# A message-passing network on one core: one of four one-hot comparisons of a unit is made by GpSimd instead of VectorE

## The reference, cut to what matters

```python
def gcn_conv(x, edge_index, W, b):
    xw = x @ W.T
    deg = jax.ops.segment_sum(jnp.ones_like(dst, dtype=x.dtype), dst, num_segments=n)
    dinv = jnp.where(deg > 0, jax.lax.rsqrt(deg), 0.0)
    norm = dinv[src] * dinv[dst]
    msg = xw[src] * norm[:, None]
    out = jax.ops.segment_sum(msg, dst, num_segments=n)
    return out + b
```

## Time and profile before

| | |
|---|---|
| median of three runs | 5927.08 us |
| the profiled execution | 5925.47 us, span 5923.7 us |
| the stage `build_counts_and_sum` | from 138.2 to 771.7 us, 633.5 us |
| VectorE, TensorE, ScalarE, GpSimd busy over the whole span | 55%, 55%, 41%, 39% |
| granted clock of TensorE over the span | 0.749 of full speed |

### The profile page before, as it was taken

The page is one execution under the profiler, slowest core; times in us unless marked ns, Lnnn a source line. Parts: engine busy times, 40 slices in busy tenths (PEclk is TensorE's granted clock), DMA queues, the critical chain, the costliest instruction groups (busy, mean ns, idle before and its releaser), DMA issues. The chain is left out here.

```text
span 5923.7 us, 64720 instructions
## 1 busy us (share of the span) xinstructions
PE 3257.2 (55%) x16208; PEld 1977.8 (33%) x16208; DVE 3247.8 (55%) x10115; ACT 2411.6 (41%) x5229; POOL 2310.7 (39%) x2409
## 2 busy tenths in 40 slices
PE   2887887514555555562255555555523555565563
PEld 1333353303333333341133333333311334333342
DVE  6998953504544545585155555555822455454576
ACT  1766620114434444443244443444433444443453
POOL 3000002173455454415445445444064545545422
PEclk7999998756777777786577777777756777777786
DMA  2111124221122111101111111111021111112110
GB/s 74 59 59 78 59 84 166 85 62 34 46 47 48 44 46 44 45 22 44 38 47 47 45 47 46 46 46 43 4 53 37 46 45 47 46 45 47 46 25 23
DMA packets 127649, 298.66 MB, mean 50 GB/s; under 512 B 45413, under 2 KB 74973, under 8 KB 123713
## 3 DMA queue, kind: packets, MB, share of 16 engines
q0 software_dynamic: 74976, 155.58, 11.4%
q1 hardware_dynamic: 52320, 139.24, 7.1%
HBM read 241.28 MB, written 53.38 MB: 50 GB/s over the span
## 5 line engine op out<-in xcount | busy, mean ns | idle before, releaser
L1399 POOL DMA_INDIRECT work<-table,lane_src x2184 | 2071.5, 948 | 1992.4 <-PE psum L1553 1100.5
L1496 PE MATMUL psum<-work 128*128 128x396 bf16 (+1 forms) x5850 | 1445.0, 395 | 844.1 <-issue 624.5
L1438 ACT ACTIVATE work<-work,middle_node_number 128x384 f16<-128x384 f16 x1587 | 958.1, 604 | 2003.8 <-DMA work<-table,lane_src 711.7
L1714 DVE TENSOR_TENSOR node_sums<-node_sums,psum 128x136 f32 x2418 | 592.6, 294 | 1444.1 <-remote 854.9
L1553 PE MATMUL psum<-work 128*128 128x136 f32 x4836 | 830.6, 337 | 847.6 <-DVE node_sums L1714 659.9
L1496 PEld LDWEIGHTS psum<-work 128*128 128x128 bf16 x5850 | 649.4, 113 | 1475.2 <-issue 997.0
L1553 PEld LDWEIGHTS psum<-work 128*128 128x128 f32 x4836 | 773.3, 239 | 959.1 <-issue 795.3
L1441 ACT ACTIVATE work<-work 128x384 bf16<-128x384 f16 x1587 | 829.4, 523 | 51.8
L715 PE MATMUL psum<-work 128*128 128x448 f16 x2100 | 460.0, 357 | 48.1 <-DVE node_sums L709 44.9
L744 DVE TENSOR_SCALAR work<-work 128x400 f16<-128x400 f16 x1568 | 462.5, 315 | 0.0
L772 PE MATMUL psum<-work 128*128 128x400 f16 x1568 | 340.3, 341 | 112.0 <-DVE work L744 90.2
(11 more groups left out here) (360 smaller groups left out, 2573.5 us busy)
## 6 DMA issues: line engine op xcount, KB each, us to landing
counts<-work SPq DMA_DIRECT2D x14, 2800.0 KB, 8.2
work<-counts SPq DMA_DIRECT2D x14, 2800.0 KB
work<-table,lane_src POOLq DMA_INDIRECT x2184
work<-spread SPq DMA_DIRECT2D x78, 256.0 KB
work<-masks SPq DMA_DIRECT2D x78, 128.0 KB
work<-source_rows SPq DMA_DIRECT2D x39, 192.0 KB
spread<-node_sums SPq DMA_DIRECT2D x4, 896.0 KB
table<-work SPq DMA_DIRECT2D x10, 330.0 KB
```

The source lines that it names most:

```text
L1399: pool.indirect_dma_start(m.ring[:, s % SLOTS, 0:F + H], None, m.d_table[H], bass.IndirectOffsetOnAxis(ap=m.src[:, s:s + 1], axis=0)).then ...
L1438: act.activation(away, rows_of(g, u), ACT.Abs, bias=m.low_tile[:, hi:hi + 1]).then_inc(far_known, 1)
L1496: mm = pe.matmul(aid_banks[:, k, 0:3 * (F + H)], hot_of(g, u)[:, k * P:(k + 1) * P], m.all_thirds[:, :, hi, 0:F + H], start=(hi == 0), sto ...
L1714: dve.tensor_tensor(to, to, sum_slot(s), ALU.add).then_inc(summed, 1)
```

## The change

VectorE makes `hot_lo` of tiles 0 and 1 only. GpSimd gets a program in this block: 392 comparisons, one per unit, for tile 2, written out one behind another with constant positions and constant waits. It waits for `unit_done` as VectorE does and raises a new semaphore, `next_low_onehot`, for each; TensorE waits for that too before a unit.

```diff
@@ build_counts_and_sum, VectorE
-                        if b < CB - 1:
+                        if b < CB - 2:
                             dve.tensor_scalar(m.hot_lo[:, d, b, :], m.iota_cols[:, 0:P], m.low[:, b, bass.ds(n, 1)], None, ALU.is_equal)
                         t = dve.tensor_scalar(m.hot_key[:, d, b, :], m.iota_cols[:], m.key[:, b, bass.ds(n, 1)], None, ALU.is_equal)
@@ GpSimd
+        @block.gpsimd
+        def _(pool):
+            for n in range(CUNITS):
+                if n >= DEPTH:
+                    pool.wait_ge(unit_done, n - (DEPTH - 1))
+                pool.tensor_scalar(m.hot_lo[:, n % DEPTH, CB - 2, :], m.iota_cols[:, 0:P], m.low[:, CB - 2, n:n + 1], None, ALU.is_equal
+                                   ).then_inc(lo_pool, 1)
+            pool.wait_ge(lo_pool, CUNITS)
@@ TensorE
                     pe.wait_ge(hot, n + 1)
                     pe.wait_ge(lo_hot, n + 1)
+                    pe.wait_ge(lo_pool, n + 1)
```

More of the change, by code:

```diff
@@ L721, in build_counts_and_sum @@
 def build_counts_and_sum(nc, m):
-    ph, (hot, lo_away, lo_hot, unit_done, evacuated, stored0, stored1, produced, summed) = phase(
-        nc, "onehots_done", "last_low_distance", "last_low_onehot", "unit_counted", "unit_evacuated", "chunk_stored_0", "chunk_stored_1", "chunk_product", "unit_summed")
+    ph, (hot, lo_away, lo_hot, lo_pool, unit_done, evacuated, stored0, stored1, produced, summed) = phase(
+        nc, "onehots_done", "last_low_distance", "last_low_onehot", "next_low_onehot", "unit_counted", "unit_evacuated", "chunk_stored_0", "chunk_stored_1", "chunk_product", "unit_summed")
     stored = (stored0, stored1)
```

## The result

| | before | after |
|---|---|---|
| median | 5928.01 us (5918.64 to 5931.12) | 5882.92 us (5879.45 to 5884.45) |
| ratio | | 0.9926, 95% interval 0.9909 to 0.9943 |
| the profiled execution's span | 5923.7 us | 5882.6 us |
| the stage, first to last 400-column comparison | 633.2 us | 581.9 us |

The stage alone gained 51.3 us.

What follows compares the result with a forecast made beforehand. VectorE was taken as the bound at 1.50 us a unit. Per unit 0.31 - 0.02 - 0.04 - 0.163 gave +0.087 us, times 392 +34 us, so 5927 + 34 = 5961 us; range 5885 to 6040.

Steps and rivals of the forecast that it cites:

- The bound: In the stage VectorE never stops, 1.50 us a unit; TensorE needs 1.24 us and waits for it.
- The removed part: One 128-column VectorE comparison L743 per unit goes: 392 x 0.163 = 64 us.
- GpSimd and TensorE at no cost of their own: GpSimd's 392 comparisons and TensorE's extra wait were costed at nothing, GpSimd being idle and up to four units ahead.
- That the two engines get into each other's way: VectorE's comparisons and GpSimd's instructions take turns, whole instructions at a time; this decides the sign.
- GpSimd's duration: GpSimd's 128-column comparison takes 0.26 + 108 x 1.66 ns = 0.44 us undisturbed.
- The term h: Time GpSimd's comparison keeps VectorE out, per unit: 0.31 us, ends 0.16 and 0.49, break-even 0.22.
- my range: Kernel time from 5885 to 6040 us; the ends worked from 0.16 and 0.49 us of lockout were 5871 and 6063.
- The lower end: Lockout 0.16 us, smaller loss, whole shadow of the sum: -0.143 us a unit, -56 us, 5871 us.
- The shadow of the sum: GpSimd's turn may run beside VectorE's small sum L709, freeing 0.08 us; half counted, 0.04 us a unit.
- Rival 2: Cheap turns, 0.16 to 0.2 us, in the sum's shadow: -12 to -56 us, say 5895; one in seven.
- a correction of 0.06 to 0.02: VectorE's loss against the lockout time: 0.06 us less by L744, 0.02 more by L529; middle taken, 0.02 less.
- The stalls at the loop's branch: About 50 us of stalls at chunk ends and the loop's branch, 39.9 before L709; the change does not touch them.

Runs made afterwards that it cites:

- sum_early: Changed kernel with VectorE's small sum L709 moved from the unit's end to behind tile 1's 400-column comparison; ratio 0.9976 to the kernel before, stage 602.1 us.
- the addition: Kernel before plus GpSimd adding two inputs of 640 single-precision columns into spare memory, nobody waiting for it; stage 1094.2 us.
- changed_again: Changed kernel, nothing altered, timed again; ratio 0.9869, stage 582.2 us, in a group where the kernel before takes 4392 us.
- changed_third: Changed kernel, nothing altered, timed beside the kernel where GpSimd makes tiles 1 and 2; ratio 0.9912, median 5947.11 us, stage 582.3 us.

## Why the prediction was wrong, step by step

- **The bound: right.** VectorE sets the pace, each unit 1.50 us before and 1.36 after, TensorE fits beside it.
- **The removed part: right.** 64 us forecast, 64.5 in the stage and 64 at the end when nobody makes the comparison.
- **GpSimd and TensorE at no cost of their own: right.** TensorE waits 5.5 us for GpSimd.
- **That the two engines get into each other's way: right** in kind. Comparisons of both are stretched.
- **GpSimd's duration: too small.** 0.60 us undisturbed, not 0.44. A column costs (1.27 - 0.60) / 272 = 2.5 ns and not the 1.66 of the two-input rows. This alone would have moved the forecast further up.
- **The term h: the step that failed.** "So h = 0.31" set the time in which VectorE is shut out equal to GpSimd's duration less its start. That holds for two inputs of 640 columns (1.15 to 1.36 us lost, as the earlier trace rows say), not for one input of 128. One turn costs 0.10 us in all, the working's h less 0.02, against 0.29. Both ends of my range came from durations too, so the range missed with it. The lower end, h = 0.16, was nearest: with its smaller loss and the whole shadow it comes to the same -0.143 us a unit as the runs, for a reason that did not hold, since it took a GpSimd instruction of 0.29 us and the real one lasts 0.60.
- **The shadow of the sum: right mechanism, half the size.** I took 0.04 us, half of 0.08; the turn falls beside the sum in most units, and 0.08 are hidden. sum_early, which only moves the sum, loses 20 us of the stage.
- With both put right the sum is 0.10 - 0.08 - 0.163 = -0.143 us for 336 units and 0.10 - 0.163 = -0.063 for 56: -52 us, where the stage shows -51.
- **Rival 2** ("cheap turns ... in the shadow of the sum: say 5895") is what happened. It had one in seven. Its mechanism and place were right, and its weight was too low since I took a pair of long two-input instructions for the nearest row. The transfers beside L529 had shown a loss of 0.14 us beside an instruction of 0.95, and L529 is the only VectorE instruction in those rows that has the form at issue. That row said that a loss need not follow the duration, and I read it as one of two values for a correction of 0.06 to 0.02.
- **The stalls at the loop's branch: wrongly named**, without effect on the result. They belong to the register loads: one of the longest is spent in such a load, and with 28 registers they grow from 39.5 to 114.6 us. Why a load is longest at the start of a pass through the loop is not explained.

## What to carry to other kernels

Work for GpSimd beside a busy VectorE is priced by what VectorE loses, not by how long GpSimd's instruction lasts: 0.60 us of GpSimd took 0.10 us or 0.02 from VectorE and saved it 0.163. Keep the piece short, since the loss grew from 0.07 to 0.51 us between 128 and 400 columns and reached 1.36 of 1.53 us for the addition, and let it fall beside something of VectorE that isn't disturbed, here the small sum from PSUM. Read a price from a row of the same form, and if there is none, put the instruction into spare memory and measure that before arguing a sign.

## What the runs showed of the hardware that I had not expected

- GpSimd's 16-bit comparison of 128 columns is 0.60 us long and that of 400 is 1.27, while VectorE loses 0.07 and 0.51 us to them; 128 columns of 32 bits cost both engines the same as 16-bit ones.
- In the first 56 units of the changed kernel's first trace, where VectorE makes comparison after comparison and no sum, single GpSimd comparisons last up to 2.20 us, and three in a row 5.64, while VectorE loses only 0.09 us a unit. In changed_again and changed_third, the same kernel, none of them lasts over 0.90 us in that stretch and VectorE loses 0.10. So the stretching comes and goes from one execution to another, and VectorE's loss doesn't depend on it; what sets it was not found.

```profile
149.34 5.64 POOL L765 TENSOR_SCALAR work<-work 128x128 f16<-128x128 f16 x3
```

- A load of registers on VectorE takes 0.96 us for 4, 1.03 for 7, 1.3 for 14 and 6.24 for 28 at the least, and up to 8.0 us for 14 and 12 us for 28. Why it grows like that, and why it is longest at the start of the loop's pass, stays open.
